# A graph network of four layers: part of the degree sums goes to GpSimd, and totals are summed in quarters of TensorE's array

## The chip, the cores and the metric

One core of a Trainium2 chip. The metric is the device time of one execution in microseconds; the kernel before takes 1945.23 (median of 3 runs, 1944.27 to 1945.79).

## What is computed

`adj` is 8192 x 8192, `x` 8192 x 64, all float32. Each of four layers normalises x, multiplies by adj, and adds the result to x:

```
h = relu(layernorm(x));  x = x + adj @ dropout(h)
h = relu(layernorm(x));  x = x + normalise(relu([h, (adj@h + h) / max(deg + 1, 1)] @ W1 + b))
h = relu(layernorm(x));  x = x + D(adj + I)D @ h @ W2,   D = (deg + 1)^-1/2
h = relu(layernorm(x));  x = x + [h, adj@h / (deg + 1)] @ W3.T
```

with deg the row sums of adj. The degrees are needed first at the end of layer 1 (the second layer), and the sum over adj's columns must be made while adj passes by.

## The kernel before

adj is 256 MB and is cut into 16 x 16 units of 1 MB, a unit (b, g) being the block of output row b and source g, held as 128 x 2048. There are 16 output rows of 512 nodes. SyncE loads the units in one written-out order (`LOADS`) into a ring of 12 slots, and the diagonal units into two slots of their own. A slot is loaded again when TensorE and, in the first pass, VectorE have let its unit go.

The first pass (phase 1) reads all 256 units, one output row after another. In row b the units with source g > b are multiplied for layer 0 only (`alone`: 4 matmuls of 512 columns, in two halves of the array, written to partitions 0 to 63 and 64 to 127). Units with g < b serve layers 0 and 1 (`both`), since the states of those sources are ready. In the order of loads: 15-b single units, b-1 double ones, the diagonal, the unit (b, b-1). In row b, behind its first unit, `finish(0, b-1)` multiplies the sums of row b-1 by a weight into Z, and VectorE makes new states of it (`end_layer_0`, after the fifth add of row b) and adds one on the diagonal (`add_one`). TensorE waits for both at the diagonal of row b.

The row sums of adj: VectorE adds the units of a row into `row_sum` (`sum_unit`, line 944), the diagonal second to last (`sum_diag`, 950), and folds the 2048 columns into 1024 of `row_total` (`fold`, 955). TensorE sums over partitions with a matmul whose weights are zero but for one column of ones (`picker`), so that row b's sum lands in partition b of each half of the bank `DEG` (`count_total`, 577). In rows 0 to 5 TensorE also sums 6, 5, 4, 3, 2 and 1 units directly (`count_unit`, 569). At row 15 the degrees are copied out, turned and taken by VectorE (`turn_degrees`, 586; `degrees`, 976). GpSimd only sets up constants and zeroes, and later issues the stores.

Phases 2 to 4 re-read parts of adj for the later layers and don't touch the sums. A printed matmul of the trace is half of a float32 matmul of the program: `alone` shows as 8 and `both` as 16.

Of the kernel before, what the change touches and what calls it, by code (L numbers as in the profile page):

```python
# [16 lines left out]
QUARTERS = 4  # L17
HEAD = 4

LAYERS = 4  # L20
P_DROP = 0.1
LN_EPS = 1e-5
# [5 lines left out]

SINGLES = [list(range(LAST, b, -1)) for b in range(ROWS)]

PE_SUMS = [SINGLES[b][1:7 - b] for b in range(6)] + [[]] * (ROWS - 6)
DVE_SUMS = [[g for g in SINGLES[b] + list(range(b)) if g not in PE_SUMS[b]] for b in range(ROWS)]


FIRST_A = (((3, 1), (1, 1)), ((3, 2), (2, 1)), ((3, 3), (2, 2)))
# [83 lines left out]

FREED = {key: n for n, key in enumerate(units_let_go())}  # L120
SUMMED = {key: n for n, key in enumerate((1, b, g) for b in range(ROWS) for g in DVE_SUMS[b])}

PROLOGUE = (3, 2, 1, 0)

# [5 lines left out]
def gnn_stack(nc, x_in, u_in, stream_in, w1_in, b1_in, w2_in, w3_in, x_out):  # L130
# [6 lines left out]
    with ctx:  # L137
        def sbuf(name, shape):
            return ctx.enter_context(nc.sbuf_tensor(name, shape, fp32))
# [4 lines left out]
        def sem(name):  # L144
            return ctx.enter_context(nc.semaphore(name))
# [7 lines left out]
        y = sbuf("y", [P, ROWS * COLS])  # L153
        u = y[:, 2 * FEATS:2 * FEATS + TILES * F]
        row_sum = sbuf("row_sum", [P, UNIT])
        row_total = [sbuf(f"row_total{i}", [P, 2 * COLS]) for i in range(2)]
        z_sb = sbuf("z_sb", [P, FEATS])
        centred = sbuf("centred", [P, FEATS])
        squares = sbuf("squares", [P, FEATS])
        scaled = [sbuf(f"scaled{i}", [P, FEATS]) for i in range(2)]  # L160
        ident = sbuf("ident", [P, P])
        picker = sbuf("picker", [P, 2 * F - 1])
        degree_rows = sbuf("degree_rows", [P, COLS])
        below = sbuf("below", [P, LAYERS, F])
        bias = sbuf("bias", [P, F])
# [36 lines left out]
        z_done = sem("z_done")  # L202
        z_taken = sem("z_taken")
        total_ready = sem("total_ready")
        total_counted = sem("total_counted")
        deg_copied = sem("deg_copied")
        deg_turned = sem("deg_turned")
        deg_taken = sem("deg_taken")
# [81 lines left out]
        @block.sync  # L290
        def _(sp):
            quarter = TILES * F // QUARTERS
            for q in PROLOGUE:
                part = slice(q * quarter, (q + 1) * quarter)
                sp.dma_start(x[:, part], x_in[:, part]).then_inc(xu_loaded[q], 16)
                sp.dma_start(u[:, part], u_in[:, part]).then_inc(xu_loaded[q], 16)
            for key in LOADS:
                if key[0] == "diag":
                    n = DIAGS[key]
                    if n >= 2:  # L300
                        sp.wait_ge(diag_freed, n - 1)
                    sp.dma_start(diag[n % 2][:, :], stream_in[key[2], key[2]]).then_inc(diag_loaded[n % 2], 16)
                else:
                    n = PLACE[key]
                    if n >= RING:
                        before = RING_LOADS[n - RING]
                        sp.wait_ge(*freed(before))
                        if before in SUMMED:
                            sp.wait_ge(unit_summed, SUMMED[before] + 1)
                    sp.dma_start(ring[n % RING][:, :],  # L310
                                 stream_in[key[1], key[2]]).then_inc(unit_loaded[n % RING], 16)

        @block.gpsimd
        def _(gp):
            nc.gpsimd.memset(own_y(LAST, 1), 0.0).then_inc(gp_step, 1)
            gp.wait_ge(gp_step, 1)
            nc.gpsimd.memset(ident[:, :], 0.0)
            nc.gpsimd.memset(picker[:, :], 0.0)
            nc.gpsimd.memset(below[:, 0, :], 0.0).then_inc(gp_step, 1)
            gp.wait_ge(gp_step, 2)  # L320
            nc.gpsimd.memset(picker[:, F - 1:F], 1.0)
# [5 lines left out]
            gp.wait_ge(gp_step, 3)  # L327
            nc.gpsimd.affine_select(out=below[:, 0, :], in_=below[:, 0, :], compare_op=ALU.not_equal,
                                    fill=1.0, base=-F, pattern=[[-1, F]],
                                    channel_multiplier=1).then_inc(consts_ready, 1)  # L330


            gp.wait_ge(z_done, rank(1, LAST) + 1)
            nc.gpsimd.memset(own_y(LAST, 1), 0.0).then_inc(last_zeroed, 1)

            for b in ORDER[3]:
                gp.wait_ge(h_ready, QUARTERS + rank(3, b) + 1)
                gp.dma_start(x_out[:, b * FEATS:(b + 1) * FEATS], own(x, b)).then_inc(out_stored, 16)
            gp.wait_ge(out_stored, 16 * ROWS)

        @block.scalar
        def _(act):
# [64 lines left out]
            for b in range(ROWS):  # L407
                if b > 0:
                    norm_root()
                if b == LAST:  # L410
                    act.wait_ge(total_counted, ROWS)
# [95 lines left out]
        def _(pe):  # L507
# [35 lines left out]
            def finish(layer, b):  # L543
# [10 lines left out]
                if layer == 2 and b == LAST:  # L554
                    pe.wait_ge(last_zeroed, 1)
                if n >= 1:
                    pe.wait_ge(z_taken, n)
                for t in range(TPR):
# [1 line left out]
                                            start=True, stop=True)  # L560
                mm_z.then_inc(z_done, 1)

            def count_unit(key):

                b = key[1]
                pick = picker[:, F - 1 - b:2 * F - 1 - b]
                for k in (0, 2):
                    for half in range(2):
                        nc.tensor.matmul(DEG[half * F:(half + 1) * F, :], pick, source_tile(slot(key), k + half),  # L569
                                         start=key == (1, 0, PE_SUMS[0][0]) and k == 0, stop=False)  # L570

            def count_total(b):

                pick = picker[:, F - 1 - b:2 * F - 1 - b]
                pe.wait_ge(total_ready, b + 1)
                for half in range(2):
                    mm_d = nc.tensor.matmul(DEG[half * F:(half + 1) * F, :], pick,  # L577
                                            row_total[b % 2][:, half * COLS:(half + 1) * COLS],
                                            start=False, stop=b == LAST)
                mm_d.then_inc(total_counted, 1)  # L580

            def turn_degrees():

                pe.wait_ge(deg_copied, 1)
                for t in range(TPR):
                    mm_d = nc.tensor.matmul(HT[:, t * ROWS:(t + 1) * ROWS], degree_rows[:, t * P:(t + 1) * P],
                                            below[:, 0, 0:ROWS], start=True, stop=True)
                mm_d.then_inc(deg_turned, 1)

            def turn_own(layer, b):  # L590
# [53 lines left out]
            for b in range(ROWS):  # L644
# [2 lines left out]
                    pe.wait_ge(*gathered(0, b - 2))  # L647
                for i, g in enumerate(SINGLES[b]):
                    await_unit((1, b, g), 0)
                    if g in PE_SUMS[b]:  # L650
                        count_unit((1, b, g))
                    alone((1, b, g), 0, low, high, i == 0, False, b > 0 and g == b + 1)
                    if i == 0 and b > 0:
                        finish(0, b - 1)
                        count_total(b - 1)
                if b >= 2:
                    pe.wait_ge(part_copied, PARTS.index((1, b - 2)) + 1)
                for g in range(b - 1):
                    await_unit((1, b, g), 0, 1)
                    both((1, b, g), 0, low, b == LAST and g == 0, g == 0, False, False)  # L660
                    if b == LAST and g == 0:
                        finish(0, b - 1)
                        count_total(b - 1)
                    if b == LAST and g == 10:
                        count_total(LAST)
# [149 lines left out]
        def _(dve):  # L815
# [132 lines left out]
            def sum_diag(b):  # L948
                dve.wait_ge(*diag_arrived(1, b))
                chain(nc.vector.tensor_tensor(row_sum[:, :], row_sum[:, :], diag_slot(1, b)[:, :], ALU.add))  # L950

            def fold(b):
                if b >= 2:
                    dve.wait_ge(total_counted, b - 1)
                nc.vector.tensor_tensor(row_total[b % 2][:, :], row_sum[:, 0:2 * COLS], row_sum[:, 2 * COLS:4 * COLS],
                                        ALU.add).then_inc(total_ready, 1)
                dve.wait_ge(total_ready, b + 1)

# [14 lines left out]

            def degrees():
                dve.wait_ge(deg_turned, 1)
                nc.vector.tensor_scalar(degree[:, :].rearrange("p (b t) -> p t b", t=TPR),
                                        HT[:, 0:TILES].rearrange("p (t b) -> p t b", t=TPR),
                                        1.0, None, ALU.add).then_inc(deg_taken, 1)
# [40 lines left out]
            for b in range(ROWS):  # L1019
                units = [(1, b, g) for g in DVE_SUMS[b]]  # L1020
                count_first = units[0]
                for i, key in enumerate(units[1:], 1):
                    if i == 1:
                        dve.wait_ge(*loaded(count_first))
                    if i == len(units) - 1:
                        sum_diag(b)
                    sum_unit(key, i)
                    if i == 5 and b > 0:
# [78 lines left out]
```

## Time and profile before

| | |
|---|---|
| median of 3 runs | 1945.23 us |
| profiled execution, own time | 1944.17 us |
| its span, mean granted clock | 1942.4 us, 0.999 |
| TensorE busy | 1905.4 us (98%) |
| VectorE busy | 854.9 us (44%), most of it in the first 750 us |
| GpSimd busy | 11.3 us (1%) |
| HBM read | 667.03 MB, 344 GB/s over the span |

The span runs from the first instruction to the last. Busy shares are means over stages with different limits; the first pass ends near 765 us, and what is changed lies in it. A time in microseconds at the head of a row is counted from the span's start.

### The profile page before, as it was taken

The page shows a single profiled execution, that of the slowest core. Times are in us where ns is not written, and L with a number is a line of the kernel's source. Part 1 is how long each engine was busy: PE and PEld are TensorE (multiplying, and loading weights), DVE is VectorE, ACT ScalarE, POOL GpSimd, SP SyncE. Part 2 cuts the span into 40 slices and gives each one's busy share as a digit, 9 for nine tenths or more (in the row PEclk, how much of TensorE's full clock was granted, in tenths as well). Part 3 has the DMA queues.
Part 4 walks back from the last instruction along what each step waited for, and adds up shares of the span by engine and source line. Part 5 has one row for each costly group of instructions (what it writes and reads, how often), then busy time and mean ns, then how long its engine had stood idle before and what let it go on. Part 6 is the DMA issues. An engine that isn't in the chain of part 4 may idle for free.

```text
span 1942.4 us, 17859 instructions
## 1 busy us (share of the span) xinstructions
PE 1905.4 (98%) x7216; PEld 751.6 (39%) x7216; DVE 854.9 (44%) x1023; ACT 115.1 (6%) x293; POOL 11.3 (1%) x29
## 2 busy tenths in 40 slices
PE   5999999999999999999999999999999999999998
PEld 2333333333333333344444444344444444344333
DVE  8678999988877763622112111321211110110322
ACT  0000000000000001100000000111000000000000
POOL 0000000000000000000000000000000000000000
PEclk9999999999999999999999999999999999999999
DMA  9999999998888875498888888397999989999998
GB/s 383 421 421 421 421 420 421 421 415 349 344 320 315 309 290 215 170 372 291 293 298 287 300 297 287 150 400 287 399 382 368 347 304 422 376 360 415 353 422 337
DMA packets 93632, 670.30 MB, mean 345 GB/s; under 512 B 11120, under 2 KB 11120, under 8 KB 12656
## 3 DMA queue, kind: packets, MB, share of 16 engines
q1 hardware_dynamic: 92160, 666.94, 87.4%
q0 software_dynamic: 768, 2.10, 0.3%
q8 instruction: 59, 0.97, 0.2%
q10 hardware_dynamic: 624, 0.13, 0.0%
q14 instruction: 21, 0.17, 0.0%
HBM read 667.03 MB, written 2.10 MB: 344 GB/s over the span
## 4 chain that ended last, share of the span: by engine, by line
PE 90%; DVE 7%; DMA 2%; issue 1%; ACT 0%; SPq 0%; POOL 0%; DVEq 0%
PE acc L509 48%; PE acc L538 36%; PE Z L559 3%; PE DEG L569 1%; DMA ring<-stream_in 1%; PE DEG L577 1%; DMA diag<-stream_in 1%; DVE inverse L846 1%; DVE mean L842 1%; PE HT L600 1%; DVE states L886 0%; DVE z_sb L878 0%; DVE squares L845 0%; DVE centred L843 0%; ACT rooted L358 0%
## 5 line engine op out<-in xcount | busy, mean ns | idle before, releaser
L509 PE MATMUL acc<-ring,states 128*64 128x512 f32 x4160 | 919.5, 594 | 29.0 <-DMA ring<-stream_in 21.2
L538 PE MATMUL acc<-ring,states 128*128 128x512 f32 x1792 | 778.8, 594 | 0.0
L509 PEld LDWEIGHTS acc<-ring,states 128*64 128x64 f32 x4160 | 297.4, 137 | 605.2 <-issue 595.5
L538 PEld LDWEIGHTS acc<-ring,states 128*128 128x128 f32 x1792 | 337.3, 190 | 414.0 <-issue 414.0
L944 DVE TENSOR_TENSOR row_sum<-row_sum,ring 128x2048 f32<-128x2048 f32 x187 | 428.5, 2292 | 9.0 <-DMA ring<-stream_in 3.8
L878 DVE TENSOR_TENSOR z_sb<-Z,deg_rsqrt 128x256 f32<-128x256 f32 x16 | 6.8, 425 | 337.2 <-PE Z L559 337.1
L911 DVE TENSOR_TENSOR y<-acc,y 64x512 f32<-64x512 f32 x16 | 11.1, 691 | 282.3 <-PE acc L538 274.9
L509 PE MATMUL acc<-diag,states 128*64 128x512 f32 x448 | 103.6, 595 | 0.0
L374 ACT COPY y<-acc 64x512 f32<-64x512 f32 x45 | 26.1, 580 | 1023.1 <-PE acc L509 748.6
L559 PEld LDWEIGHTS Z<-below,y 128*128 128x128 f32 x512 | 62.9, 191 | 50.6 <-issue 15.0
L1005 DVE TENSOR_TENSOR y<-acc,y 64x512 f32<-64x512 f32 x36 | 24.6, 683 | 111.7 <-PE acc L509 111.4
L559 PE MATMUL Z<-below,y 128*128 128x64 f32 x512 | 69.6, 279 | 2.2 <-DVE y L1006 2.2
L509 PEld LDWEIGHTS acc<-diag,states 128*64 128x64 f32 x448 | 31.6, 137 | 66.9 <-issue 66.6
L971 DVE TENSOR_TENSOR diag<-diag,ident 128x384 f32<-128x384 f32 x12 | 6.7, 558 | 106.5 <-ACT row_sum L393 106.4
L944 DVE TENSOR_TENSOR row_sum<-ring 128x2048 f32<-128x2048 f32 x16 | 36.7, 2292 | 31.1 <-DMA ring<-stream_in 30.2
L894 DVE TENSOR_TENSOR x<-Z,x 128x256 f32<-128x256 f32 x16 | 6.8, 425 | 78.2 <-PE Z L559 77.9
L569 PE MATMUL DEG<-ring,picker 128*64 128x512 f32 x168 | 39.8, 594 | 0.0
L950 DVE TENSOR_TENSOR row_sum<-row_sum,diag 128x2048 f32<-128x2048 f32 x16 | 36.7, 2293 | 2.4 <-DMA diag<-stream_in 1.9
L381 ACT COPY y<-HT 64x256 f32<-64x256 f32 x64 | 23.4, 365 | 159.4 <-PE HT L600 159.0
L358 ACT ACTIVATE rooted<-to_root 128x4 f32<-128x4 f32 (+1 forms) x68 | 14.0, 206 | 315.0 <-DVE to_root L832 286.9
L842 DVE TENSOR_REDUCE mean<-x 128x4 f32<-128x256 f32 (+1 forms) x52 | 25.0, 481 | 7.7 <-DMA y<-u_in 6.0
L1006 DVE TENSOR_TENSOR y<-acc,y 64x512 f32<-64x512 f32 x36 | 24.9, 692 | 1.3
(77 smaller groups left out, 374.3 us busy)
## 6 DMA issues: line engine op xcount, KB each, us to landing
ring<-stream_in SPq DMA_DIRECT2D x604, 1024.0 KB, 8.6
diag<-stream_in SPq DMA_DIRECT2D x28, 1024.0 KB, 10.4
x<-x_in SPq DMA_DIRECT2D x4, 512.0 KB, 7.2
y<-u_in SPq DMA_DIRECT2D x4, 512.0 KB, 9.1
x_out<-x POOLq DMA_DIRECT2D x16, 128.0 KB, 5.8
below<-w_in ACTq DMA_DIRECT2D x6, 16.0 KB, 6.2
bias<-b_in ACTq DMA_DIRECT2D x1, 32.0 KB, 10.9
```

The costliest lines, as they stand in the source:

```text
L374: nc.scalar.copy(own_y(b, 1 if layer == 2 else 0), half_of(bank, half)).then_inc(part_copied, 1)
L381: done = nc.scalar.copy(by_parity[:, parity], turned)
L509: return nc.tensor.matmul(half_of(bank, half), h[layer % 2][:, J], moving, start=start, stop=stop)
L538: done = nc.tensor.matmul(acc[bank][:, :], states[:, J * 2 * F:(J + 1) * 2 * F], source_tile(slot(key), k), start=first and k == 0, stop=l ...
L559: mm_z = nc.tensor.matmul(Z[:, t * F:(t + 1) * F], own_y(b)[:, t * P:(t + 1) * P], below[:, layer, :], start=True, stop=True)
L569: nc.tensor.matmul(DEG[half * F:(half + 1) * F, :], pick, source_tile(slot(key), k + half), start=key == (1, 0, PE_SUMS[0][0]) and k == 0, ...
L577: mm_d = nc.tensor.matmul(DEG[half * F:(half + 1) * F, :], pick, row_total[b % 2][:, half * COLS:(half + 1) * COLS], start=False, stop=b = ...
L842: chain(nc.vector.tensor_reduce(m, by_tile(xs), X, ALU.add))
L944: nc.vector.tensor_tensor(row_sum[:, :], before, slot(key)[:, :], ALU.add).then_inc(unit_summed, 1 if count > 1 else 2)
L950: chain(nc.vector.tensor_tensor(row_sum[:, :], row_sum[:, :], diag_slot(1, b)[:, :], ALU.add))
L1005: chain(nc.vector.tensor_tensor(own_y(r, 0), half_of(bank, 0), own_y(r, 0), ALU.add))
L1006: nc.vector.tensor_tensor(own_y(r, 0), half_of(bank, 1), own_y(r, 0), ALU.add).then_inc(group_folded, 1)
```

## The change

- `count_unit` and `PE_SUMS` go. GpSimd adds 8 units of row 0 (the first eight) and 5 of each of rows 1 to 8 (positions 1, 4, 7, 10 and 13) into `pool_sum`, a stretch of y that is free until then. VectorE adds the other units, then `pool_sum`, then the diagonal and the last unit. GpSimd starts on row b when VectorE has taken row b-1's `pool_sum`. SyncE waits for GpSimd too before it reloads such a slot.
- The fold has two steps, to 1024 and to 512 columns. There are four `row_total` arrays. TensorE sums four rows at once (`count_totals`): each of four 32-wide quarters of the array takes one row's total, in rows 4, 8 and 12 behind the third unit, and at the end of row 15.
- The degrees come out in another order, so they are turned with `chosen` in place of `below`, and VectorE takes them with four instructions instead of one.
- The zeroing of the last block of y follows GpSimd's sums.

```diff
-PE_SUMS = [SINGLES[b][1:7 - b] for b in range(6)] + [[]] * (ROWS - 6)
+POOL_ROWS = 9
+POOL_SUMS = [SINGLES[0][:8]] + [(SINGLES[b] + list(range(b)))[1:15:3] for b in range(1, POOL_ROWS)]
+DVE_SUMS = [[g for g in SINGLES[b] + list(range(b)) if b >= POOL_ROWS or g not in POOL_SUMS[b]] ...]
...
+        pool_sum = y[:, ROWS * COLS - UNIT:ROWS * COLS]
-        row_total = [sbuf(f"row_total{i}", [P, 2 * COLS]) for i in range(2)]
+        row_total = [sbuf(f"row_total{i}", [P, COLS]) for i in range(QUAD)]
...
+                        if before in POOLED:
+                            sp.wait_ge(pool_summed, POOLED[before] + 1)
...
+            for b in range(POOL_ROWS):
+                first, *others = [(1, b, g) for g in POOL_SUMS[b]]
+                if b > 0:
+                    gp.wait_ge(pool_taken, b)
+                gp.wait_ge(*loaded(first))
+                for i, key in enumerate(others):
+                    gp.wait_ge(*loaded(key))
+                    before = pool_sum if i else slot(first)[:, :]
+                    nc.gpsimd.tensor_tensor(pool_sum, before, slot(key)[:, :],
+                                            ALU.add).then_inc(pool_summed, 1 if i else 2)
+                    gp.wait_ge(pool_summed, POOLED[key] + 1)
...
-            def count_unit(key):
-            def count_total(b):
+            def count_totals(q):
+                pe.wait_ge(total_ready, QUAD * (q + 1))
+                for j in range(QUAD):
+                    mm_d = nc.tensor.matmul(DEG[j * QUARTER:(j + 1) * QUARTER, :],
+                                            picker[:, QUARTER - 1 - q:2 * QUARTER - 1 - q], row_total[j][:, :],
+                                            start=q == 0, stop=q == QUAD - 1)
...
-                    if g in PE_SUMS[b]:
-                        count_unit((1, b, g))
                     alone((1, b, g), 0, low, high, i == 0, False, b > 0 and g == b + 1)
+                    if i == 2 and b > 0 and b % QUAD == 0:
+                        count_totals(b // QUAD - 1)
                     if i == 0 and b > 0:
                         finish(0, b - 1)
-                        count_total(b - 1)
...
+            def sum_pool(b):
+                dve.wait_ge(pool_summed, POOLED[1, b, POOL_SUMS[b][-1]] + 1)
+                nc.vector.tensor_tensor(row_sum[:, :], row_sum[:, :], pool_sum, ALU.add).then_inc(pool_taken, 1)
...
             def fold(b):
+                chain(nc.vector.tensor_tensor(row_sum[:, 0:2 * COLS], row_sum[:, 0:2 * COLS],
+                                              row_sum[:, 2 * COLS:4 * COLS], ALU.add))
+                if b >= QUAD:
+                    dve.wait_ge(totals_counted, b // QUAD)
+                nc.vector.tensor_tensor(row_total[b % QUAD][:, :], row_sum[:, 0:COLS], row_sum[:, COLS:2 * COLS],
```

## Rows read from the trace of the kernel before

**Rows 1.** Stretches: length, busy us of PE, PEld, DVE, ACT, POOL; clock, DMA share, GB/s.

```profile
60.00:120.00 60.00, 59.48 (x284) 20.89 (x284) 38.40 (x27) 3.10 (x6) 0.00 (x0) 1.00 1.01 421
...
240.00:300.00 60.00, 60.00 (x286) 20.59 (x284) 58.51 (x38) 1.95 (x4) 0.00 (x0) 1.00 1.01 421
```

**Rows 2.** The page's chain that ended last, shares by engine.

```profile
PE 90%; DVE 7%; DMA 2%; issue 1%; ACT 0%; SPq 0%; POOL 0%; DVEq 0%
```

**Rows 3.** The chain in order of time: start, us, engine and line.

```profile
80.05 24.03 PE acc L509 x112
...
401.96 44.63 PE acc L509 x208
...
1116.43 41.20 PE acc L538 x96
```

**Rows 4.** Groups by line and form, 0 to 830 us.

```profile
L944 DVE TENSOR_TENSOR row_sum<-row_sum,ring 128x2048 f32<-128x2048 f32 x187 | 428.5, 2292 | 9.0 <-DMA ring<-stream_in 3.8
...
L569 PE MATMUL DEG<-ring,picker 128*64 128x512 f32 x168 | 39.8, 594 | 0.0
...
L577 PE MATMUL DEG<-row_total,picker 128*64 128x512 f32 x64 | 17.2, 616 | 0.5 <-DVE row_total L955 0.5
```

**Rows 5.** TensorE's instructions in order of time, 225 to 320 us.

```profile
228.59 1.11 PE L559 MATMUL Z<-below,y 128*128 128x64 f32 x8
229.63 1.08 PE L577 MATMUL DEG<-row_total,picker 128*64 128x512 f32 x4
230.53 1.89 PE L569 MATMUL DEG<-ring,picker 128*64 128x512 f32 x8
...
270.12 1.10 PE L559 MATMUL Z<-below,y 128*128 128x64 f32 x8
271.15 1.08 PE L577 MATMUL DEG<-row_total,picker 128*64 128x512 f32 x4
...
311.65 1.10 PE L559 MATMUL Z<-below,y 128*128 128x64 f32 x8
```

**Rows 6.** VectorE's instructions in order of time, 225 to 320 us.

```profile
224.91 2.29 DVE L944 TENSOR_TENSOR row_sum<-ring 128x2048 f32<-128x2048 f32 x1 [1.79 <-DMA ring<-stream_in]
...
234.83 2.29 DVE L944 TENSOR_TENSOR row_sum<-row_sum,ring 128x2048 f32<-128x2048 f32 x1 [0.19 <-DMA ring<-stream_in]
...
262.28 1.23 DVE L955 TENSOR_TENSOR row_total<-row_sum 128x1024 f32<-128x1024 f32 x1
...
275.23 0.42 DVE L894 TENSOR_TENSOR x<-Z,x 128x256 f32<-128x256 f32 x1
...
279.43 18.57 DVE L944 TENSOR_TENSOR row_sum<-row_sum,ring 128x2048 f32<-128x2048 f32 x8
```

**Rows 7.** GpSimd's groups by line and form, whole span.

```profile
L315 POOL MEMSET y<- 64x512 f32 x1 | 0.5, 519 | 0.3 <-POOLq L1100 0.3
...
L322 POOL TENSOR_SCALAR_AFFINE_SELECT ident<-ident 128x128 f32<-128x128 f32 x1 | 0.3, 282 | 0.1
...
L317 POOL MEMSET ident<- 128x128 f32 x1 | 0.2, 204 | 0.1
```

**Rows 8.** All engines in order of time, 0 to 75 us.

```profile
20.34 3.68 PE L509 MATMUL acc<-ring,states 128*64 128x512 f32 x8 [20.34 <-DMA ring<-stream_in]
...
39.48 2.28 DVE L944 TENSOR_TENSOR row_sum<-ring 128x2048 f32<-128x2048 f32 x1
...
62.24 1.23 DVE L955 TENSOR_TENSOR row_total<-row_sum 128x1024 f32<-128x1024 f32 x1
```

**Rows 9.** VectorE at 749 and 783 us, and GpSimd's one zeroing beside it.

```profile
749.23 0.27 DVE L976 TENSOR_SCALAR degree<-HT 128x64 f32<-128x64 f32 x1 [11.95 <-PE HT L586]
749.53 0.20 DVE L980 TENSOR_SCALAR deg_clipped<-degree 128x64 f32<-128x64 f32 x1
...
783.70 0.43 DVE L915 TENSOR_TENSOR z_sb<-z_sb,bias 128x256 f32<-128x256 f32 x1
...
L334 POOL MEMSET y<- x1: 519/519/519, 783.3 to 783.3; 64x512 f32 x1
```

More of the change, by code:

```diff
@@ L18 @@
 HEAD = 4
+QUARTER = 32
 LAYERS = 4
@@ L29 @@
 SINGLES = [list(range(LAST, b, -1)) for b in range(ROWS)]
-PE_SUMS = [SINGLES[b][1:7 - b] for b in range(6)] + [[]] * (ROWS - 6)
-DVE_SUMS = [[g for g in SINGLES[b] + list(range(b)) if g not in PE_SUMS[b]] for b in range(ROWS)]
+POOL_ROWS = 9
+POOL_SUMS = [SINGLES[0][:8]] + [(SINGLES[b] + list(range(b)))[1:15:3] for b in range(1, POOL_ROWS)]
+DVE_SUMS = [[g for g in SINGLES[b] + list(range(b)) if b >= POOL_ROWS or g not in POOL_SUMS[b]] for b in range(ROWS)]
 FIRST_A = (((3, 1), (1, 1)), ((3, 2), (2, 1)), ((3, 3), (2, 2)))
@@ L121 @@
 SUMMED = {key: n for n, key in enumerate((1, b, g) for b in range(ROWS) for g in DVE_SUMS[b])}
+POOLED = {key: n for n, key in enumerate((1, b, g) for b in range(POOL_ROWS) for g in POOL_SUMS[b])}
+QUAD = 4
 PROLOGUE = (3, 2, 1, 0)
@@ L161, in gnn_stack @@
         ident = sbuf("ident", [P, P])
-        picker = sbuf("picker", [P, 2 * F - 1])
+        picker = sbuf("picker", [P, 2 * QUARTER - 1])
+        chosen = sbuf("chosen", [P, ROWS])
         degree_rows = sbuf("degree_rows", [P, COLS])
@@ L204, in gnn_stack @@
         total_ready = sem("total_ready")
-        total_counted = sem("total_counted")
+        totals_counted = sem("totals_counted")
+        pool_summed = sem("pool_summed")
+        pool_taken = sem("pool_taken")
         deg_copied = sem("deg_copied")
@@ L314, in _ @@
         def _(gp):
-            nc.gpsimd.memset(own_y(LAST, 1), 0.0).then_inc(gp_step, 1)
-            gp.wait_ge(gp_step, 1)
             nc.gpsimd.memset(ident[:, :], 0.0)
             nc.gpsimd.memset(picker[:, :], 0.0)
+            nc.gpsimd.memset(chosen[:, :], 0.0)
             nc.gpsimd.memset(below[:, 0, :], 0.0).then_inc(gp_step, 1)
-            gp.wait_ge(gp_step, 2)
-            nc.gpsimd.memset(picker[:, F - 1:F], 1.0)
+            gp.wait_ge(gp_step, 1)
+            nc.gpsimd.memset(picker[:, QUARTER - 1:QUARTER], 1.0)
+            nc.gpsimd.affine_select(out=chosen[:, :].rearrange("p (j q) -> p j q", q=QUAD),
+                                    in_=chosen[:, :].rearrange("p (j q) -> p j q", q=QUAD),
+                                    compare_op=ALU.not_equal, fill=1.0, base=0,
+                                    pattern=[[-QUARTER, QUAD], [-1, QUAD]], channel_multiplier=1)
             nc.gpsimd.affine_select(out=ident[:, :], in_=ident[:, :], compare_op=ALU.not_equal, fill=1.0,
@@ L326, in _ @@
                                     channel_multiplier=1).then_inc(gp_step, 1)
-            gp.wait_ge(gp_step, 3)
+            gp.wait_ge(gp_step, 2)
             nc.gpsimd.affine_select(out=below[:, 0, :], in_=below[:, 0, :], compare_op=ALU.not_equal,
@@ L330, in _ @@
                                     channel_multiplier=1).then_inc(consts_ready, 1)
+            for b in range(POOL_ROWS):
[9 more added lines that the diff above has]
+                    gp.wait_ge(pool_summed, POOLED[key] + 1)
+            gp.wait_ge(pool_taken, POOL_ROWS)
+            nc.gpsimd.memset(own_y(LAST, 1), 0.0).then_inc(last_zeroed, 1)
             gp.wait_ge(z_done, rank(1, LAST) + 1)
@@ L410, in _ @@
                 if b == LAST:
-                    act.wait_ge(total_counted, ROWS)
+                    act.wait_ge(totals_counted, QUAD)
                     nc.scalar.copy(degree_rows[:, :], DEG[:, :]).then_inc(deg_copied, 1)
@@ L553, in finish @@
                     pe.wait_ge(hT_copied, TURNS.index((layer, b)) + 1)
-                if layer == 2 and b == LAST:
-                    pe.wait_ge(last_zeroed, 1)
+                if layer % 2 == 0 and b == LAST:
+                    pe.wait_ge(last_zeroed, layer // 2 + 1)
                 if n >= 1:
@@ L561, in finish @@
                 mm_z.then_inc(z_done, 1)
-            def count_unit(key):
[L565 to L570, printed above, removed]
-            def count_total(b):
[L574 to L580, printed above, removed]
+            def count_totals(q):
[4 more added lines that the diff above has]
+                                            start=q == 0, stop=q == QUAD - 1)
+                mm_d.then_inc(totals_counted, 1)
             def turn_degrees():
@@ L586, in turn_degrees @@
                     mm_d = nc.tensor.matmul(HT[:, t * ROWS:(t + 1) * ROWS], degree_rows[:, t * P:(t + 1) * P],
-                                            below[:, 0, 0:ROWS], start=True, stop=True)
+                                            chosen[:, :], start=True, stop=True)
                 mm_d.then_inc(deg_turned, 1)
@@ L662, in _ @@
                         finish(0, b - 1)
-                        count_total(b - 1)
                     if b == LAST and g == 10:
-                        count_total(LAST)
+                        count_totals(QUAD - 1)
                     if b == LAST and g == 11:
@@ L950, in sum_diag @@
                 chain(nc.vector.tensor_tensor(row_sum[:, :], row_sum[:, :], diag_slot(1, b)[:, :], ALU.add))
+            def sum_pool(b):
+                dve.wait_ge(pool_summed, POOLED[1, b, POOL_SUMS[b][-1]] + 1)
+                nc.vector.tensor_tensor(row_sum[:, :], row_sum[:, :], pool_sum, ALU.add).then_inc(pool_taken, 1)
+                dve.wait_ge(pool_taken, b + 1)
             def fold(b):
-                if b >= 2:
-                    dve.wait_ge(total_counted, b - 1)
-                nc.vector.tensor_tensor(row_total[b % 2][:, :], row_sum[:, 0:2 * COLS], row_sum[:, 2 * COLS:4 * COLS],
+                chain(nc.vector.tensor_tensor(row_sum[:, 0:2 * COLS], row_sum[:, 0:2 * COLS],
[3 more added lines that the diff above has]
+                nc.vector.tensor_tensor(row_total[b % QUAD][:, :], row_sum[:, 0:COLS], row_sum[:, COLS:2 * COLS],
                                         ALU.add).then_inc(total_ready, 1)
@@ L975, in degrees @@
                 dve.wait_ge(deg_turned, 1)
-                nc.vector.tensor_scalar(degree[:, :].rearrange("p (b t) -> p t b", t=TPR),
-                                        HT[:, 0:TILES].rearrange("p (t b) -> p t b", t=TPR),
-                                        1.0, None, ALU.add).then_inc(deg_taken, 1)
+                for t in range(TPR):
+                    taken = nc.vector.tensor_scalar(degree[:, :].rearrange("p (q j t) -> p t j q", j=QUAD, t=TPR)[:, t],
+                                                    HT[:, t * ROWS:(t + 1) * ROWS].rearrange("p (j q) -> p j q", q=QUAD),
+                                                    1.0, None, ALU.add)
+                taken.then_inc(deg_taken, 1)
                 dve.wait_ge(deg_taken, 1)
@@ L1025, in _ @@
                     if i == len(units) - 1:
+                        if b < POOL_ROWS:
+                            sum_pool(b)
                         sum_diag(b)
```

## The prediction

> **What bounds the kernel now.** I read the table of stretches first, then the shares of the chain that ended last, then its pieces in order of time, then the groups of the first 830 us, and last the instructions of TensorE, VectorE and GpSimd one by one around 225 to 312 us.
>
> The table of stretches [rows 1] shows two resources full at once in the first layer: TensorE is busy 60 us of 60 and the transfers have a share of 1.0 at 421 GB/s. The granted clock is 1.00 there, the 2.4 GHz level. VectorE goes from 38 us busy in 60 to 58.5. The chain is 90% TensorE [rows 2]. So shortening TensorE's work helps only until the next unit's landing is what it waits for.
>
> The pace of landings is seen where VectorE waits for each unit: five adds start from 224.91 to 234.83, 2.48 apart, each released by a transfer; 1.05 MB at 421 GB/s is 2.49 [rows 1, 6]. The first of them needs the third load of row 5, number 82 if a row's 16 loads are counted on from 0 (diagonal too). Load k thus lands at 20.7 + 2.49 k; load 0 by this at 20.7, and TensorE's first matmul, released by a transfer, starts at 20.34 [rows 8].
>
> TensorE's prices come from the chain [rows 3]: 112 half-width matmuls in 24.03, 0.2146 each, so a unit read for one layer (8) is 1.72, one for two layers (16) 3.43. 96 full-width ones in 41.20 are 0.429 each: half the width, side by side with its pair, is half the time. Finishing a row takes 1.04 (228.59 to 229.63) and counting one total 0.91 (229.63 to 230.53) [rows 5]. A row b is (15-b) x 1.72 + (b+1) x 3.43 + 1.04 + 0.91, plus 1.72 for each counted unit. Row 6 gives 41.4; measured, from finish to finish, 311.65 - 270.12 = 41.53 [rows 5]. Rows 1 to 5 come out near 40.6 with their counted units, against 39.8 for 16 landings. TensorE is behind the landings by little.
>
> **Taken from TensorE.** 21 counted units, 168 matmuls, 39.8 busy but 21 x 1.72 = 36 of time [rows 4]; 16 single totals, 64 matmuls, 16 x 0.91 = 14.6. Most of this is cover for transfers. Without it, row 5's first two-layer unit is load 90, landing at 244.8; four such units, diagonal and last unit are 6 x 3.43 = 20.6, so row 5 ends no earlier than 265.4. Row 6: load 105 lands at 282.2, plus 7 x 3.43 = 306.2; by its own work it would be 265.4 + 41.5 - 0.9 = 306.0. From row 7 TensorE's own work is longer. Row 7 began at 311.65 - 1.72 = 309.9 before [rows 5], so 3.7 are won there, out of the 41.5 removed up to then (36 and six totals); TensorE waits for landings in the other 38. Ten totals are counted later, 9.1.
>
> **Added to TensorE.** Four quarter-width counts of 8 matmuls each. Between both ends: all four side by side 8 x 0.429 / 4 = 0.86, one after another 3.43 [rows 3]. The halves do run side by side, so I take 0.86. Three of the counts lie after row 7: 2.6, at most 10.3. Net gain if all else is hidden: 3.7 + 9.1 - 2.6 = 10.2; with quarters one by one, 2.5.
>
> **VectorE.** An add of a unit is 2.29, with its gap 2.32 [rows 4]. In rows 1 to 8 nine unit adds, GpSimd's sum and the diagonal are 11 x 2.32 = 25.5, the fold in two steps 1.25 + 0.67 = 1.9 (one step is 1.23 for 1024 elements), states and diagonal 4.2 (275.23 to 279.43) [rows 6]: 31.6, under 39.8. Alone it is no bound. From row 9 it has 15 adds and 40.9 a row, under TensorE's 45.8 and more. The degrees take four instructions for one of 0.27, some 0.6 more; TensorE has a two-layer unit of 3.43 to do before it needs what VectorE makes there, five steps like the two of 0.27 and 0.20 [rows 9], so nothing; uncovered it would cost 0.6. The zeroing of the last block (0.52) and the constants lie beside the prologue [rows 7], also nothing.
>
> **GpSimd.** 7 adds in row 0, then 4 in each of eight rows. No row shows such an add. Writing 64x512 takes 0.52 and 128x128 0.20: 0.82 ns an element; the select on 128x128 also reads and takes 0.28, 0.6 ns an element more [rows 7]. For 2048 elements: 1.8 if reads hide, 3.0 with one read on top, 4.3 with two; 5.1 if three passes go at 0.82. I take 4.3, since the select's read did not hide. The Trainium skill (GPSIMD Engine Reference, "Elementwise — side-by-side cycle accounting") gives 4497 ns for this add at this size, which would put 31 adds 6 us higher in the case forecast; no trace here has one.
>
> If it runs beside VectorE it is hidden: 17 of a row's 40. Its last unit is load 13; it is ready at load 14's landing + 1.8, VectorE's three adds follow, and the ring slots are wanted 12 loads later.
>
> **Beside or in turns.** The disputed cost. VectorE's adds read two arrays of SBUF, and so do GpSimd's. The only overlap in the trace is a zeroing at 783.3 that only writes, and VectorE's addition of two SBUF arrays at 783.70 took 0.43, no more than 256 elements of it do elsewhere (0.42) [rows 6, 9]. For two readers the bounds are: no loss, or each waits for the whole of the other's instruction. I take turns, a judgement: the case seen excludes only a loss from writing, and all 31 new instructions read. The Trainium skill (SBUF — State Buffer, "SBUF: two separate sides") says that a VectorE instruction with two SBUF inputs and a GpSimd one that reads SBUF exclude each other for whole instructions; no run yet shows it, and by it the sum is the one below.
>
> In turns a row costs 31.6 + 4 x 4.3 + 8 changes of engine at some 0.1 = 49.6, over 39.8. Row 0: the first add of sums is at 39.48 now [rows 8]; the seven GpSimd adds start near 23 and put 30.1 into it. They hide VectorE's one-input steps of the two prologue quarters left, each quarter two of 1024 elements at 1.25 (a fold's 1.23 and its gap) and some 0.8 of small ones: 6.6. So 63. Eight adds and the fold, 20.5, and the three first GpSimd adds of row 1, 12.9: row 0's total is ready at 97 (now 63.5 [rows 8]). Row 7's total: 97 + 7 x 49.6 = 444.
>
> Who waits: SyncE for the slots of added units, with all later loads behind it; and the new count of totals 4 to 7 stands in row 8 behind its third unit, and everything of TensorE is queued behind it. After 444 come 0.9, four units at 1.72 and nine pieces at 3.43: 38.7. Row 9 would start at 483; it starts at 401.96 - 0.91 - 1.04 - 1.72 = 398.3 now [rows 3]. That is 85 late. Afterwards TensorE's work (45.7 and more a row) exceeds VectorE's 40.9, so the delay stays, less eight totals (7.3), plus two counts (1.7): +79. The layers behind are full of TensorE work with no more slack [rows 2], so it reaches the end. Span 1942.4 + 79 = 2021.5; the profiled execution's own time is 1944.17, 1.8 over its span and 1.1 under the median 1945.23: **2023**. With GpSimd's add at 3.0 a row is 44.4, row 0 at 84, the end 1974; at 5.1, 2054.
>
> **Rivals.**
> - *Both engines add side by side: faster.* TensorE, VectorE and the transfers work at once today and VectorE's add keeps its 2.29, which speaks for it [rows 1, 4]; that GpSimd is not among them, against. Then -10.2: 1935 (to 1942 if the quarters go one by one). It decides once VectorE and GpSimd together take under 39.8 a row, so from a loss of under 8 us a row.
> - *They share by element*, so that only part of a GpSimd add is lost: rows of 41 to 44, 1950 to 1975.
> - *The change takes TensorE work away to no effect*: side by side, but quarters one by one, or a GpSimd add over 6.5: row 0's seven then end past 68.7, and the last slot that they hold is wanted by load 20, which should land at 70.5. 1942.
>
> **How the numbers follow.** Turns 0.58 (1974 to 2054), sharing by element 0.07, side by side 0.29 (1932 to 1939), no effect 0.06. Under 0.2% (3.9 us) a measurement can't tell from no change. Faster 0.30, same 0.05, slower 0.65. The range must hold both signs: 1933 to 2045, with the likeliest's own at 1974 to 2045 mostly.
>
> **What the profile after would show.** If turns: VectorE adds that start late, or last longer, while GpSimd's run; rows 1 to 8 near 50 apart by the folds; transfers well under 421 GB/s there for want of ring slots; a long wait of TensorE at the count in row 8. If side by side: adds of 2.29, rows 39.8 apart, TensorE waiting on landings for some 38 us in rows 0 to 6, each count 0.9. The forecast is wrong if two readers don't disturb one another; its size is wrong if GpSimd's add is far from 4.3, or if TensorE's granted clock falls during the new waits, which would add a few us.

## The result, and the profile after

The changed kernel takes 2014.42 us (median of 5 runs, 2012.55 to 2016.61) against 1944.67 for the kernel before: ratio 1.036, 95% interval 1.0348 to 1.0372. It is slower by 70 us. The profiled execution took 2016.5 with a span of 2014.7; its mean granted clock is 0.976, where it was 0.999.

The stretches of the changed kernel, columns as in [rows 1] (in all rows PE is TensorE, DVE VectorE, POOL GpSimd and SPq SyncE's queue):

```profile
60.00:120.00 60.00, 40.17 (x174) 13.65 (x172) 58.39 (x34) 1.58 (x4) 23.57 (x4) 0.89 0.73 295
...
420.00:480.00 60.00, 46.80 (x216) 15.11 (x214) 58.66 (x31) 1.95 (x4) 19.19 (x5) 0.89 0.78 317
480.00:540.00 60.00, 60.00 (x284) 20.53 (x282) 56.60 (x44) 2.15 (x5) 0.00 (x0) 1.00 0.94 378
```

TensorE falls from 59.5 busy to 40.2 in the first of these, the transfers from 421 to 295 GB/s, and VectorE rises from 38.4 to 58.4 with work taken from it. From 480 us on, when GpSimd adds nothing more, TensorE is full again. What SyncE's queue waits for before its loads shows why the transfers fall: it waits 324.1 us for VectorE to let a slot go, where it was 97.5 before, and 32.8 for GpSimd. The first row is of the kernel before, the other two of the changed one:

```profile
SPq L309 <- DVE row_sum L944: 97.5, 38, 18.4
```

```profile
SPq L319 <- DVE row_sum L963: 324.1, 72, 12.4
...
SPq L321 <- POOL y L357: 32.8, 7, 5.2
```

The page's chain that ended last:

```profile
PE 71%; DVE 26%; DMA 1%; issue 1%; ACT 0%; POOL 0%; SPq 0%; DVEq 0%
```

VectorE had 7% of it [rows 2]. The groups, columns as in [rows 4]:

```profile
L963 DVE TENSOR_TENSOR row_sum<-row_sum,ring 128x2048 f32<-128x2048 f32 x160 | 417.1, 2607 | 4.9
L357 POOL TENSOR_TENSOR y<-y,ring 128x2048 f32<-128x2048 f32 x30 | 169.4, 5647 | 82.0 <-DMA ring<-stream_in 81.1
...
L977 DVE TENSOR_TENSOR row_sum<-row_sum 128x1024 f32<-128x1024 f32 x16 | 53.2, 3328 | 0.6
```

VectorE's add has a mean of 2607 ns (2292 before), the first step of the fold 3328. A mean hides what happens; the instructions of both engines at the end of row 0, each engine's in order of time, show it (the row of 21.56 is GpSimd's first add):

```profile
79.01 2.29 DVE L969 TENSOR_TENSOR row_sum<-row_sum,diag 128x2048 f32<-128x2048 f32 x1
81.34 6.51 DVE L963 TENSOR_TENSOR row_sum<-row_sum,ring 128x2048 f32<-128x2048 f32 x1
87.88 5.44 DVE L977 TENSOR_TENSOR row_sum<-row_sum 128x1024 f32<-128x1024 f32 x1
93.36 4.88 DVE L981 TENSOR_TENSOR row_total<-row_sum 128x512 f32<-128x512 f32 x1
...
21.56 4.51 POOL L357 TENSOR_TENSOR y<-ring 128x2048 f32<-128x2048 f32 x1 [19.07 <-DMA ring<-stream_in]
...
79.20 6.50 POOL L357 TENSOR_TENSOR y<-ring 128x2048 f32<-128x2048 f32 x1 [21.12 <-DVE row_sum L973]
85.77 11.92 POOL L357 TENSOR_TENSOR y<-y,ring 128x2048 f32<-128x2048 f32 x2
```

Here the two engines go in turns. GpSimd's add is issued at 79.20, in the middle of VectorE's; it ends at 85.70, 4.4 after VectorE's end at 81.30, though it takes 4.51 where it starts freely. VectorE's add of 81.34 takes 6.51 = 2.29 + 4.22; the folds behind it 5.44 = 1.23 + 4.21 and 4.88 = 0.69 + 4.19. Nothing runs at half speed: each instruction waits for one whole instruction of the other engine. (A wait at this place counts as busy time, so the view of waits doesn't have it.) The Trainium skill's rule (SBUF — State Buffer, "SBUF: two separate sides") says just this, and the trace agrees. The 4.51 also agrees with the 4497 ns that the Trainium skill gives for this add (GPSIMD Engine Reference, "Elementwise — side-by-side cycle accounting").

Row totals are ready when line 981 ends. Its instructions in rows 1, 2 and 7 of the changed kernel:

```profile
141.07 0.69 DVE L981 TENSOR_TENSOR row_total<-row_sum 128x512 f32<-128x512 f32 x1
188.76 0.69 DVE L981 TENSOR_TENSOR row_total<-row_sum 128x512 f32<-128x512 f32 x1
...
429.10 4.87 DVE L981 TENSOR_TENSOR row_total<-row_sum 128x512 f32<-128x512 f32 x1
```

From 93.36 (row 0) to 429.10 (row 7) are 335.7, 48.0 a row, where a row was 40.4 between 262.28 and 302.69 before (the first of these stands in [rows 6]). TensorE in row 8:

```profile
434.02 1.94 PE L598 MATMUL DEG<-row_total,picker 128*32 128x512 f32 x8 [13.21 <-DVE row_total L981]
435.88 31.96 PE L540 MATMUL acc<-ring,states 128*64 128x512 f32 x144
...
476.36 1.10 PE L590 MATMUL Z<-below,y 128*128 128x64 f32 x8
```

It waits 13.21 at the count, gets going at 434.02, and starts row 9 one unit before 476.36, at 474.6; before it was 398.3 [rows 3]. That is 76.3 late. The count takes 1.86 here at a granted clock of 0.50 (1.2 GHz), to which it fell in the wait (it was 1.00 from 417 to 420). It stays there until after 437, so the first units behind the count are slowed too; columns as in [rows 1]:

```profile
434.00:435.00 1.00, 0.98 (x8) 0.20 (x8) 0.95 (x1) 0.00 (x0) 0.00 (x0) 0.50 0.00 0
...
437.00:438.00 1.00, 1.00 (x6) 0.17 (x4) 1.00 (x1) 0.00 (x0) 0.00 (x0) 0.69 0.29 33
438.00:439.00 1.00, 1.00 (x8) 0.36 (x6) 0.97 (x2) 0.00 (x0) 0.00 (x0) 1.00 0.86 352
```

In row 12, at 1.00 (2.4 GHz), the same eight matmuls take 1.00, from 623.58 to 624.58:

```profile
623.58 1.07 PE L598 MATMUL DEG<-row_total,picker 128*32 128x512 f32 x8
624.58 3.65 PE L540 MATMUL acc<-ring,states 128*64 128x512 f32 x16
```

### The profile page after: what moved, and what is told of

The parts are those of the page before. It is cut to its first block, busy times and chain, and to the rows that moved or that the text cites. A ratio compares the mean times of both kernels' runs of the same rounds, so it can differ in the third digit from the quotient of the medians.

```text
span 2014.7 us, 17551 instructions
## 1 busy us (share of the span) xinstructions
PE 1887.1 (94%) x7016; PEld 740.0 (37%) x7016; DVE 979.2 (49%) x1024; ACT 115.3 (6%) x293; POOL 237.3 (12%) x70
## 4 chain that ended last, share of the span: by engine, by line
PE 71%; DVE 26%; DMA 1%; issue 1%; ACT 0%; POOL 0%; SPq 0%; DVEq 0%
PE acc L569 35%; PE acc L540 33%; DVE row_sum L963 11%; PE Z L590 2%; DVE row_sum L977 2%; DVE centred L862 1%; DMA ring<-stream_in 1%; DVE row_sum L973 1%; DVE row_sum L969 1%; DVE row_total L981 1%; DVE inverse L865 1%; DVE mean L861 1%; DVE states L883 1%; DVE row_sum L862 1%; PE HT L621 1%
## 5 line engine op out<-in xcount | busy, mean ns | idle before, releaser
L540 PE MATMUL acc<-ring,states 128*64 128x512 f32 x4160 | 929.3, 600 | 64.5 <-DMA ring<-stream_in 39.1
L963 DVE TENSOR_TENSOR row_sum<-row_sum,ring 128x2048 f32<-128x2048 f32 x160 | 417.1, 2607 | 4.9
L357 POOL TENSOR_TENSOR y<-y,ring 128x2048 f32<-128x2048 f32 x30 | 169.4, 5647 | 82.0 <-DMA ring<-stream_in 81.1
L930 DVE TENSOR_TENSOR y<-acc,y 64x512 f32<-64x512 f32 x16 | 11.1, 691 | 282.3 <-PE acc L569 274.9
L540 PE MATMUL acc<-diag,states 128*64 128x512 f32 x448 | 116.8, 659 | 29.9 <-DVE diag L990 29.9
L369 POOL DMA_DIRECT2D x_out<-x x16 | 8.8, 550 | 1148.1 <-DVE x L956 1148.1
L1033 DVE TENSOR_TENSOR y<-acc,y 64x512 f32<-64x512 f32 x36 | 24.6, 683 | 112.2 <-PE acc L540 112.0
L357 POOL TENSOR_TENSOR y<-ring 128x2048 f32<-128x2048 f32 x9 | 56.4, 6269 | 139.7 <-DVE row_sum L973 120.6
L977 DVE TENSOR_TENSOR row_sum<-row_sum 128x1024 f32<-128x1024 f32 x16 | 53.2, 3328 | 0.6
L963 DVE TENSOR_TENSOR row_sum<-ring 128x2048 f32<-128x2048 f32 x16 | 49.1, 3071 | 1.4
L862 DVE SCALAR_TENSOR_TENSOR centred<-mean,x 128x256 f32<-128x256 f32 x48 | 40.1, 836 | 1.6
```

The lines of the kernel that those rows point to most:

```text
L357: nc.gpsimd.tensor_tensor(pool_sum, before, slot(key)[:, :], ALU.add).then_inc(pool_summed, 1 if i else 2)
L540: return nc.tensor.matmul(half_of(bank, half), h[layer % 2][:, J], moving, start=start, stop=stop)
L862: chain(nc.vector.scalar_tensor_tensor(out=by_tile(cen), in0=spread(m), scalar=-1.0 / F, in1=by_tile(xs), op0=ALU.mult, op1=ALU.add))
L963: nc.vector.tensor_tensor(row_sum[:, :], before, slot(key)[:, :], ALU.add).then_inc(unit_summed, 1 if count > 1 else 2)
L977: chain(nc.vector.tensor_tensor(row_sum[:, 0:2 * COLS], row_sum[:, 0:2 * COLS], row_sum[:, 2 * COLS:4 * COLS], ALU.add))
L1033: chain(nc.vector.tensor_tensor(own_y(r, 0), half_of(bank, 0), own_y(r, 0), ALU.add))
```

## The experiments

Times are medians; "before" is the kernel before on the same chip, 1944.1 to 1944.6 in all of them. The experiments ran on three chips, so that a difference of 0.5 between two of them says nothing.

**Without GpSimd's adds.** What do the quarters and the missing share of TensorE cost by themselves?

```diff
-POOL_ROWS = 9
+POOL_ROWS = 0
...
-            gp.wait_ge(pool_taken, POOL_ROWS)
+            gp.wait_ge(consts_ready, 1)
```

> The changed kernel without GpSimd's part: VectorE adds all 15 units of every row, TensorE none, totals in quarters. Turns theory (each GpSimd add takes about 4.2 us of VectorE's time): VectorE's row is 15 x 2.32 + 1.9 + 4.2 = 40.9 instead of 48.0, row 0's total is ready at 39.5 + 34.8 + 1.9 = 76, row 7's at 362.5; TensorE's wait in row 8 shrinks from 13.2 us to 2 or 3, and the time is 1942 (1938 to 1948). Rival, that the totals in quarters or TensorE's missing share of the sums is what costs: it stays above 1965.

Measured 1945.75, ratio 1.0009 (0.9999 to 1.0018). VectorE's row is 41.1, row 7's total is ready at 363.83 + 0.69 = 364.5, and TensorE waits 1.14 for it in row 8. The larger wait of this kernel is at the other count, in row 4, for the total of row 3:

```profile
200.05 1.94 PE L598 MATMUL DEG<-row_total,picker 128*32 128x512 f32 x8 [10.14 <-DVE row_total L981]
```

This kernel and the changed one differ in GpSimd's part alone. So GpSimd's 39 adds cost 2014.4 - 1945.8 = 69 us, nearly the whole loss.

**GpSimd only writes.** Each add becomes two zeroings; GpSimd's units are missing from the sums.

```diff
-                    nc.gpsimd.tensor_tensor(pool_sum, before, slot(key)[:, :],
-                                            ALU.add).then_inc(pool_summed, 1 if i else 2)
+                    nc.gpsimd.memset(pool_sum, 0.0).then_inc(pool_turn, 1)
+                    turns += 1
+                    gp.wait_ge(pool_turn, turns)
+                    nc.gpsimd.memset(pool_sum, 0.0).then_inc(pool_summed, 1 if i else 2)
```

> The changed kernel with each of GpSimd's 39 adds replaced by two zeroings of pool_sum, one after the other; the sums are then wrong by GpSimd's units, all waits are the same. It asks whether reading is what VectorE loses to. If only a GpSimd instruction that reads SBUF holds VectorE: VectorE's adds keep 2.29 beside the zeroings, rows 1 to 6 follow the landings at 39.8, and the time is that of both engines side by side, 1935 (1931 to 1940). Rival, that any GpSimd instruction on SBUF takes turns: rows of 31.6 + 8 x 1.8 = 46, near 2000.

Measured 1935.94, ratio 0.9957 (0.9942 to 0.9972). VectorE and GpSimd in order of time:

```profile
266.66 2.29 DVE L967 TENSOR_TENSOR row_sum<-row_sum,ring 128x2048 f32<-128x2048 f32 x1
268.95 1.80 POOL L359 MEMSET y<- 128x2048 f32 x1 [13.73 <-DMA ring<-stream_in]
270.87 1.81 POOL L362 MEMSET y<- 128x2048 f32 x1
271.38 2.29 DVE L967 TENSOR_TENSOR row_sum<-row_sum,ring 128x2048 f32<-128x2048 f32 x1 [2.43 <-DMA ring<-stream_in]
```

The second zeroing lasts to 272.68, over half of VectorE's add of 271.38, and both keep their durations. Over the whole run VectorE's 160 adds of this kind have a mean of 2291 ns (2292 in the kernel before, [rows 4]), and its folds are 39.8 apart (104.47 to 144.29). VectorE's semaphore waits are those of the changed kernel, so they aren't what holds it there. This run is also the rival "side by side" made real, 0.9 from its forecast of 1935, and the transfers stay at 421 GB/s from 60 to 420 us.

**GpSimd copies.** The same with two copies of the unit in place of the add (line `nc.gpsimd.tensor_copy(pool_sum, slot(key)[:, :])`); again its units are missing.

> The changed kernel with each of GpSimd's adds replaced by two copies of the unit into pool_sum (one array read, one written); the sums lack GpSimd's units. If a single read is enough to hold VectorE's two-input instructions: VectorE adds stretched by the length of a copy (about 1.8 to 3 us), rows of 31.6 + 8 x 1.8 = 46 or more, 1998 to 2030. If it takes a GpSimd instruction with two inputs: 1935.

Measured 1974.0, ratio 1.0153, below the expected range of 1998 to 2030. Both engines in order of time:

```profile
30.51 1.89 POOL L362 COPY y<-ring 128x2048 f32<-128x2048 f32 x1
...
379.63 3.96 POOL L359 COPY y<-ring 128x2048 f32<-128x2048 f32 x1 [15.76 <-DVE row_sum L977]
381.87 3.86 DVE L967 TENSOR_TENSOR row_sum<-row_sum,ring 128x2048 f32<-128x2048 f32 x1
...
385.77 2.79 DVE L981 TENSOR_TENSOR row_sum<-row_sum 128x1024 f32<-128x1024 f32 x1
```

One read is enough: VectorE's add is 2.29 + 1.57, the fold 1.23 + 1.56. A copy takes 1.89 where nothing holds it, and holds VectorE for 1.57. The row is 44.3 (344.29 to 388.60 by line 985), under the 46 expected, since 1.8 to 3 had been taken for the hold. The expectation also left row 0 as it was, but its total is ready at 81.6 for 98.2, 16.7 earlier. So the mechanism was right, and the size was too high by both.

**The count of totals later.** It stands before the diagonal in rows 4, 8 and 12, no longer behind the third unit.

```diff
-                    if i == 2 and b > 0 and b % QUAD == 0:
-                        count_totals(b // QUAD - 1)
...
+                if b > 0 and b % QUAD == 0:
+                    count_totals(b // QUAD - 1)
                 pe.wait_ge(*diag_arrived(1, b))
```

> The changed kernel with the counts of rows 4, 8 and 12 moved from behind the third unit to just before the diagonal, the in-turn adds kept. It asks what TensorE's wait for totals adds to VectorE's lateness. If row 8's wait of 13.2 us is what sets the delay: VectorE's row 7 total is still ready at 434, but TensorE has done the units by then; it waits for the diagonal's added one at 453.3, and row 9 starts near 462 instead of 474.6: 2002 (1998 to 2006). Rival, that ring slots or VectorE's pace bind in the same way: within 3 us of the changed kernel, 2012 to 2015.

Measured 2002.15, ratio 1.0301, 12.3 under the changed kernel. TensorE in row 8:

```profile
450.25 1.07 PE L598 MATMUL DEG<-row_total,picker 128*32 128x512 f32 x8
...
452.98 3.65 PE L540 MATMUL acc<-diag,states 128*64 128x512 f32 x16 [1.66 <-DVE diag L990]
...
461.71 1.10 PE L590 MATMUL Z<-below,y 128*128 128x64 f32 x8
```

The totals are there when TensorE comes; it waits 1.66 for the added one on the diagonal. Row 9 starts at 460.0 instead of 474.6. Row 7's total is ready at 428.4, not at 434 as expected: 4.2 of it is that a third hold falls on VectorE's adds behind the fold, where it stretched the fold at 429.10 in the changed kernel. Row 12's fold on VectorE now waits 13.7 for the count, as VectorE is ahead of TensorE there:

```profile
647.91 0.69 DVE L981 TENSOR_TENSOR row_total<-row_sum 128x512 f32<-128x512 f32 x1 [13.70 <-PE DEG L598]
```

**Fewer adds.** Three units a row for GpSimd in rows 1 to 8 (`[1:15:6]` for `[1:15:3]`).

> The changed kernel with three units a row for GpSimd (two adds) in rows 1 to 8 instead of five (four adds); row 0 as it is. Turns theory: VectorE's row is 31.6 + 2 x 2.32 + 2 x 4.1 = 44.4 instead of 48.0, row 7's total is ready 7 x 3.6 = 25 earlier, at 409, and the time is 2014 - 25 = 1989 (1984 to 1994). Rival, that the cost is one of each row's chain (sum of GpSimd awaited, once a row) and not of each add: VectorE's rows stay near 48 and the time within 5 us of 2014.

Measured 1981.64, ratio 1.0191, 2.4 below the expected range. VectorE's row is 43.96 (352.92 to 396.88 by line 981), 0.4 under the 44.4 worked out. The total of row 7 is ready at 397.6, not 409: row 0's is ready 8 earlier too (89.8 for 98.2), since only one of row 1's adds falls before it, no longer three. The expectation had left row 0 as it was. The rival, a price once a row whatever the adds, is out: the row shrank by 4.0.

**The same adds later.** Five units a row in rows 9, 10 and 11 only.

```diff
-POOL_ROWS = 9
-POOL_SUMS = [SINGLES[0][:8]] + [(SINGLES[b] + list(range(b)))[1:15:3] for b in range(1, POOL_ROWS)]
+POOL_AT = [9, 10, 11]
+POOL_SUMS = [(SINGLES[b] + list(range(b)))[1:15:3] if b in POOL_AT else [] for b in range(ROWS)]
```

> GpSimd's five units a row in rows 9, 10 and 11 instead of 0 to 8, where TensorE's own work takes 45.7, 47.5 and 49.2 us a row; otherwise as the kernel in which VectorE adds alone. If lateness of VectorE costs only where it passes TensorE's pace: three rows of 48.0 for VectorE against TensorE's 142 us, so 0 to 5 us over the kernel without GpSimd, 1942 to 1948, though the stretched adds of 6.5 us are there. Rival, that the adds cost wherever they are: 3 x 7.1 = 21 us more, 1960 and up.

Measured 1946.29, 0.5 over the kernel without GpSimd's adds, which is within their spreads. The folds of rows 8, 9 and 10:

```profile
413.47 4.91 DVE L981 TENSOR_TENSOR row_total<-row_sum 128x512 f32<-128x512 f32 x1
461.24 0.69 DVE L981 TENSOR_TENSOR row_total<-row_sum 128x512 f32<-128x512 f32 x1
...
508.97 0.69 DVE L981 TENSOR_TENSOR row_total<-row_sum 128x512 f32<-128x512 f32 x1
```

They are 47.8 and 47.7 apart, and the first is stretched as before. But TensorE's own rows are 45.8, 47.5 and 49.3 here, 142.6 together against 143 for VectorE, and from 365.65 on, through all of them, no matmul has idle time before it.

**Totals in quarters, TensorE's units kept.** This is the kernel before with the quarters alone.

```diff
+            for j in range(QUAD):
+                nc.gpsimd.affine_select(out=chosen[:, :], in_=chosen[:, :], compare_op=ALU.not_equal, fill=1.0,
+                                        base=-j * QUARTER, pattern=[[-1, ROWS]], ...)
...
+                pe.wait_ge(total_ready, QUAD * (q + 1))
+                for j in range(QUAD):
+                    mm_d = nc.tensor.matmul(DEG[j * QUARTER:(j + 1) * QUARTER, :],
+                                            picker[:, F - 1 - QUAD * q - j:F - 1 - QUAD * q - j + QUARTER],
+                                            row_total[j][:, :], start=False, stop=q == QUAD - 1)
```

> The kernel before with only the totals in quarters: TensorE keeps its 21 counted units, GpSimd adds nothing, totals of four rows counted at once (partition 32 j + b for row b in quarter j), the fold in two steps. 16 totals at 0.91 become four counts at 1.0 (623.58 to 624.58 in the changed kernel). If VectorE's 0.7 more a row stays hidden: rows 1 to 6 fall to the pace of landings (3.7 won at row 7), then ten totals less and three counts more, 9.1 - 3.0 = 6.1: 1935 (1933 to 1938). Rival, that VectorE, with rows of 41.6 in 6 to 8, binds: 1939 to 1943.

Measured 1936.66, ratio 0.9958 (0.9946 to 0.9970): 0.4% faster than the kernel before, and faster than the changed one. TensorE finishes row 6, one unit into row 7:

```profile
307.99 1.10 PE L574 MATMUL Z<-below,y 128*128 128x64 f32 x8
```

Row 7 starts at 306.3, where the forecast had 306.2 by landings and 306.0 by TensorE's own work. It is TensorE's own work here: it waits for no transfer in rows 2 to 6, and its finishes of rows 5 and 6 are 40.7 apart (267.32 to 307.99). VectorE's longer fold is hidden: TensorE waits for no total.

**GpSimd's adds in four pieces.** 512 columns each, nothing else changed.

```diff
+                    for c in range(TPR):
+                        part = slice(c * COLS, (c + 1) * COLS)
+                        added = nc.gpsimd.tensor_tensor(pool_sum[:, part], before[:, part], slot(key)[:, part], ALU.add)
+                    added.then_inc(pool_summed, 1 if i else 2)
```

> The changed kernel with each of GpSimd's adds written as four of 512 columns, nothing else changed. It asks what the turns are counted in. If one whole instruction holds the other engine: a VectorE add is stretched by about 1.1 to 1.3 us at a time instead of 4.2, several in a row, and the total held per row stays 4 x 4.1 or grows by the starts, rows of 48 to 50, 2014 to 2028. Rival, that the hold lasts for all GpSimd work that is queued: stretches of 4.2 as before. Rival, that a short instruction slips in between at no cost: rows well under 48, under 1995.

Measured 1988.42, ratio 1.0225: 26 under the changed kernel, where 0 to 14 over it was expected. The time is that of the last rival, "under 1995", but not for its reason, as VectorE in order of time shows:

```profile
125.69 3.24 DVE L965 TENSOR_TENSOR row_sum<-row_sum,ring 128x2048 f32<-128x2048 f32 x1
128.97 2.18 DVE L979 TENSOR_TENSOR row_sum<-row_sum 128x1024 f32<-128x1024 f32 x1
131.18 1.65 DVE L983 TENSOR_TENSOR row_total<-row_sum 128x512 f32<-128x512 f32 x1
```

Each of them is held by 0.95, one piece, so the turn is one instruction: neither all that GpSimd has queued, nor nothing. GpSimd's pieces in the view by line, their shortest, median and longest in ns:

```profile
L359 POOL TENSOR_TENSOR y<-ring x36: 1257/2251/3325, 22.6 to 404.3; 128x512 f32<-128x512 f32 x36
```

The shortest piece takes 1.25 and holds for 0.95; the whole add takes 4.51 and holds for 4.22; the copy takes 1.89 and holds for 1.57. Each holds for 0.3 less than it takes by itself, so four pieces can hold 3.8 in place of 4.2. The row is 45.3 (357.91 to 403.25 by line 983), against 47.7 in the changed kernel (332.80 to 380.48 by line 981). Added up over these two rows, VectorE's instructions are stretched by 13.5, of 15.2 that sixteen pieces could hold, and by 15.9, of 16.9 for four whole adds. So 1.7 of the 2.4 is the shorter hold, and the rest is hold that falls where VectorE isn't held. Row 0's total is 11.7 earlier (86.5), row 7's 29.1 (404.9), and row 9 starts 27.8 earlier.

## Why the prediction was right

The forecast was 2023, the profiled execution took 2016.5 and the median is 2014.4. The range of 1933 to 2045 holds both signs, so that the time lies in it says little; what came true is the likeliest case, turns, and the path by which it costs time. Point by point:

- *Two readers go in turns.* Right, and shown from both sides: zeroings leave VectorE alone, copies and adds don't, and the hold follows the length of the one instruction (4.22, 1.57 and 0.95, for 4.51, 1.89 and 1.25). That it was turns and not the rivals was a judgement with a chance of 0.58, as no row of before had two readers at once.
- *The hold.* Taken as 4.3 with 0.1 at each change of engine, 4.5 in all. It is 4.2, and a row 48.0 for 49.6. This is the mis-sized term: 7 rows of 1.6 are 11, so row 7's total came at 434.0, not 444; row 0's at 98.2, forecast 97.
- *Where the 4.3 came from.* It is near by luck. Its working put 1.2 on top of a pure write (1.8) for each array read. A zeroing does take 1.80, but the copy, one read, takes 1.89 where 3.0 was worked out, and the add, two reads, 4.51: the first read costs 0.1 and the second 2.6. Had the change used one-input instructions, the same working would have been too high by over half.
- *Who waits.* TensorE waited in row 8 at the count, as forecast. Moving the count gives 12.3 back. That run shows the limit of the point: of 69 us the place of the count is 12, and VectorE's lateness the rest, since the diagonal waits for it next. The forecast named only the count in row 8. In the trace TensorE also waits 12.35 at row 4's count (242.30), and in rows 1 to 3 and 5 to 7 for the one that VectorE adds on the diagonal, 9.93 at most (213.97). SyncE's waits for VectorE, 324.1 us, are the slots that were forecast.
- *What comes after.* 38.7 were expected from the total to row 9, 40.6 were needed: the count of 1.86 at the fallen clock for 0.9, and 1 more. Of that, 0.8 is the clock again: the 144 matmuls behind the count take 31.96, and 31.12 without GpSimd's adds, where the clock hadn't fallen. The forecast had named a fall of the clock as something that would add to it, and left it out of the sum. The delay of 76.3 at row 9 ended as 72.3; 7.3 of totals less two counts of 1.0 would give 5.3 back, 4.0 came.
- *The lateness costs only where VectorE passes TensorE.* The forecast said that the delay stops growing at row 9; the late rows show it, 12 adds for 0.5 us.
- *TensorE's saved work is worth little.* The parts, each alone: the quarters -7.9 (1936.66 to 1944.56), dropping TensorE's 21 units +9.1 (1945.75 from 1936.66, on two chips), GpSimd's adds +68.7. Dropping 36 us of TensorE's work made the kernel slower, since VectorE got the units, six of them in row 0: row 3's total is ready at 200.0, and TensorE waits 10.14 for it at row 4's count, where it waits for nothing at 192.89 with its units kept. That one wait is nearly the whole loss: the finish of row 4 is 10.1 later (236.75 against 226.65), that of row 6 8.4 (316.37 against 307.99). Whether the later count would give it back without GpSimd's adds wasn't run.
- *A quarter-width count.* Taken at 0.86, measured 1.00: four side by side.
- *The rival of both side by side*, 1935, is what the writing run gives, 1935.9, and the point where it decides, a held row under 39.8, was never near: the shortest held row is 43.96.
- *A wrong sum that did no harm.* The forecast has rows 1 to 5 "near 40.6 with their counted units". By its own prices they are 41.5, and the finishes of before at 145.54, 187.06 and 228.59 are 41.5 apart. The 306.2 and the 309.9 for row 7 don't use it.

## What to carry to other kernels

Before work goes to a free engine, ask what it reads through. In these runs VectorE's adds of two SBUF arrays and GpSimd's instructions that read SBUF cost nearly the sum of their times, so handing over an add of 2.32 for one that holds 4.2 loses 1.9 us each. GpSimd's zeroing cost VectorE nothing, and its adds cost nothing in the end in rows where TensorE's own work is as long as VectorE's with the holds. And a count that waits for the slower engine should stand as late in the queue as its next user allows; that alone gave 12.3 here.

## What the runs showed of the hardware

A VectorE instruction needs no two inputs to be held. Five of VectorE's rows in the changed kernel while GpSimd adds, the first two from the prologue:

```profile
38.10 1.22 DVE L865 TENSOR_REDUCE inverse<-row_sum 128x16 f32<-128x1024 f32 x1
39.35 3.10 DVE L851 TENSOR_SCALAR to_root<-inverse 128x16 f32<-128x16 f32 x1
...
109.96 0.43 DVE L913 TENSOR_TENSOR x<-Z,x 128x256 f32<-128x256 f32 x1
110.42 0.42 DVE L861 TENSOR_REDUCE mean<-x 128x4 f32<-128x256 f32 x1
110.87 3.70 DVE L862 SCALAR_TENSOR_TENSOR centred<-mean,x 128x256 f32<-128x256 f32 x1
```

The reductions keep their times (1.22, 0.42), and so does the add whose other input is in PSUM (0.43). The tensor_scalar of 16 elements takes 3.10 where it takes 0.17 alone, and the step with mean and x, both in SBUF, 3.70 for 0.42. None of the held two shares an array with GpSimd's adds, so it isn't a conflict over one array. The Trainium skill (SBUF — State Buffer, "SBUF: two separate sides") names two-port modes beside two inputs; the tensor_scalar fits that, though no run here isolates it. GpSimd's copy or add held VectorE for 0.3 less than it takes by itself in each of the three cases seen, which is why four pieces of an add held less than one whole add.
